# Moving the small steps of the normalisation to GpSimd and splitting the low parts straight from PSUM

## What is computed

```python
h = relu(layernorm(x))                                   # eps 1e-5
D = adj.sum(axis=1);  s = (D + 1e-9) ** -0.5
x = x + relu((adj * s[:, None] * s[None, :]) @ h @ W.T + b)
h = relu(layernorm(x))
g = layernorm(relu(adj @ h @ gcn_w + gcn_b)) * ln_g + ln_b
# mamba(g): 256 inner channels, 16 states
xc, z = split(g @ w_in);  u = silu(conv4(xc) + conv_b)
dbc = u @ w_xp                                           # 8 ranks, 16 B, 16 C
dt = softplus(dbc[:, :8] @ w_dt + b_dt)
h_t = exp(dt * A) * h_(t-1) + dt * B * u                 # along the 8192 rows
y = (sum over states of h_t * C + u * D_skip) * silu(z)
x = x + y @ w_out
```

## Time and profile before

| | us |
|---|---|
| median of 3 runs (lowest, highest) | 2611.35 (2610.81, 2611.61) |
| the profiled execution's own time | 2612.32 |
| its span, first to last instruction | 2610.5 |
| busy: PE / DVE / ACT / POOL | 2222.9 / 2085.1 / 978.6 / 1067.6 |
| chain that ended last | PE 55%, DVE 24%, DMA 8%, issue 8%, ACT 4% |

### The profile page before, as it was taken

How to read it: one execution, slowest core, us unless ns; L and a number is a source line. 1 busy time by engine, 2 the same in 40 slices (tenths; PEclk the granted TensorE clock), 3 DMA queues, 4 the chain that set the end, 5 groups by cost and what they waited for, 6 DMA issues and landing times.

```text
span 2610.5 us, 21684 instructions
## 1 busy us (share of the span) xinstructions
PE 2222.9 (85%) x6736; PEld 1251.9 (48%) x6736; DVE 2085.1 (80%) x2087; ACT 978.6 (37%) x1696; POOL 1067.6 (41%) x461
## 2 busy tenths in 40 slices
PE   0436889999999999999999988889988988886776
PEld 0212334444457888888885434444444443443333
DVE  7899998888527656656652599999999999999997
ACT  0100000000015555555551455555555555555552
POOL 0000000000000000000000499999999999998554
PEclk9968899999999999999999989999999999997898
DMA  9999999989756556555556656665656565562221
GB/s 393 417 421 422 421 418 387 391 360 381 276 214 237 207 201 225 189 215 201 198 181 243 240 202 220 207 215 214 214 204 227 206 223 194 215 210 69 69 73 53
DMA packets 108322, 642.99 MB, mean 246 GB/s; under 512 B 14224, under 2 KB 15024, under 8 KB 42672
## 3 DMA queue, kind: packets, MB, share of 16 engines
q1 hardware_dynamic: 92160, 604.02, 61.4%
q10 hardware_dynamic: 16048, 37.57, 4.0%
HBM read 625.28 MB, written 16.25 MB: 246 GB/s over the span
## 4 chain that ended last, share of the span: by engine, by line
PE 55%; DVE 24%; DMA 8%; issue 8%; ACT 4%; DVEq 0%; ACTq 0%; SPq 0%
PE ps L848 21%; PE ps L767 14%; PE ps L888 10%; DVE ps L685 6%; DVE arena L590 6%; DMA ring<-adj 5%; DVE arena L700 5%; PE ps L966 4%; DVE ring L700 3%; DMA arena<-adj 2%; PE ps L917 2%; PE ps L909 1%; PE ps L970 1%; DVE parts L726 1%; PE ps L928 1%
## 5 line engine op out<-in xcount | busy, mean ns | idle before, releaser
L458 POOL TENSOR_TENSOR rstd<-base,minus_half 128x8 f32<-128x8 f32 (+1 forms) x40 | 84.7, 2118 | 1406.4 <-DVE base L510 811.7
L848 PE MATMUL ps<-adj_parts,h_parts 128*128 128x512 f32 x2592 | 593.6, 390 | 2.6 <-ACT adj_parts L1062 2.2
L888 PE MATMUL ps<-ring,diag_h 128*128 128x512 f32 x1152 | 566.2, 627 | 0.9 <-DVE arena L672 0.9
L848 PEld LDWEIGHTS ps<-adj_parts,h_parts 128*128 128x128 f32 x2592 | 484.7, 188 | 109.0 <-ACT adj_parts L1062 4.7
L590 DVE TENSOR_TENSOR arena<-arena,ring 128x2048 f32<-128x2048 f32 x180 | 412.6, 2292 | 57.9 <-DMA ring<-adj 47.2
L767 PE MATMUL ps<-ring,arena 128*128 128x512 f32 x824 | 381.9, 622 | 53.1 <-DMA ring<-adj 53.0
L474 POOL TENSOR_TENSOR arena<-arena 128x1024 f32<-128x1024 f32 x156 | 377.6, 2431 | 67.7 <-ACT state L1129 67.6
L700 DVE TENSOR_TENSOR_SCAN arena<-arena,state,ps 128x512 f32<-128x512 f32 x312 | 382.4, 1267 | 28.6 <-ACT arena L1137 8.7
L888 PEld LDWEIGHTS ps<-ring,diag_h 128*128 128x128 f32 x1152 | 229.5, 201 | 254.1 <-issue 248.9
L609 DVE TENSOR_TENSOR adj_parts<-ring,adj_parts 128x1024 fp32r<-128x1024 f32 x216 | 264.0, 1225 | 94.5 <-ACT adj_parts L1062 83.7
L1137 ACT ACTIVATE arena<-arena,a_sb 128x512 f32<-128x512 f32 x512 | 338.4, 708 | 0.4
(11 more groups left out here) (97 smaller groups left out, 2095.5 us busy)
## 6 DMA issues: line engine op xcount, KB each, us to landing
ring<-adj SPq DMA_DIRECT2D x452, 1024.0 KB, 6.6
arena<-c_scratch SPq DMA_DIRECT2D x128, 512.0 KB, 4.2
diag_h<-adj SPq DMA_DIRECT2D x32, 1024.0 KB, 12.6
arena<-adj SPq DMA_DIRECT2D x28, 1024.0 KB, 16.1
arena<-x ACTq DMA_DIRECT2D x16, 512.0 KB, 6.0
x_scratch<-arena ACTq DMA_DIRECT2D x8, 512.0 KB, 3.0
arena<-x_scratch ACTq DMA_DIRECT2D x16, 256.0 KB, 5.4
out<-arena ACTq DMA_DIRECT2D x16, 256.0 KB, 3.7
```

The lines of the kernel that those rows point to most:

```text
L848: last = nc.tensor.matmul(acc[:, c, :], h_parts[:, blk % 2, layer, h_part, a * F:(a + 1) * F], adj_parts[:, buf, adj_part, c * MM:(c + 1) ...
L888: last = nc.tensor.matmul((acc_c if i else y_ps)[:, c, :], tile_of(h1, JT * s + a), blk[:, a * STRIP + c * MM:a * STRIP + (c + 1) * MM], s ...
```

## The change

The additive epsilon and the product of minus mean and power leave DVE. POOL now does four steps for a normalisation: minus mean (to `nmr`), variance plus epsilon (to `base`), a wait on its own second step, the power, a wait on its own power, the product. DVE signals `base_ready` from its last `bn_aggr`, and waits for the last `norm_ready` before it overwrites `mv`. The degree's power is as before. The split of the low parts reads `dbc` in PSUM instead of `bcv` in SBUF, and frees the PSUM bank itself; ACT copies `parts` from PSUM too, then only the 32 rows of B and C to `bcv`, and waits for that copy before it issues the DMA of C. PE's waits on `parts_ready` become waits on the freed bank, and dt's matmul waits for ACT's second copy as well.

```diff
-            def power(m, cols):
+            def norm_scale(m, cols):
                 pool.wait_ge(base_ready, m + 1)
...
-                nc.gpsimd.tensor_tensor(rstd[:, 0:cols], base[:, 0:cols], minus_half[:, 0:cols],
-                                        ALU.pow).then_inc(pow_done, 1)
+                nc.gpsimd.tensor_scalar(nmr[:, 0:cols], mv[:, 0:cols, 0], -1.0, None, ALU.mult)
+                nc.gpsimd.tensor_scalar(base[:, 0:cols], mv[:, 0:cols, 1], LN_EPS, None, ALU.add)\
+                    .then_inc(pool_step, 1)
+                pool.wait_ge(pool_step, next(pool_steps))
+                nc.gpsimd.tensor_tensor(rstd[:, 0:cols], base[:, 0:cols], minus_half[:, 0:cols], ALU.pow)\
+                    .then_inc(pow_done, 1)
+                pool.wait_ge(pow_done, m + 1)
+                nc.gpsimd.tensor_tensor(nmr[:, 0:cols], nmr[:, 0:cols], rstd[:, 0:cols], ALU.mult)\
+                    .then_inc(norm_ready, 1)
...
                 step(tile_stats(tiles[taken:], taken))
+                if powers[0]:
+                    dve.wait_ge(norm_ready, powers[0])
                 for t in range(n):
                     ins = nc.vector.bn_aggr(mv[:, t, :], stats[:, t, :])
-                step(ins)
+                ins.then_inc(base_ready, 1)
                 powers[0] += 1
-                nc.vector.tensor_scalar(base[:, 0:n], mv[:, 0:n, 1], LN_EPS, None, ALU.add).then_inc(base_ready, 1)
-            def norm_bias(n):
-                dve.wait_ge(pow_done, powers[0])
-                nc.vector.scalar_tensor_tensor(nmr[:, 0:n], mv[:, 0:n, 0], -1.0, rstd[:, 0:n],
-                                               ALU.mult, ALU.mult).then_inc(norm_ready, 1)
...
                     low = parts[k % 2][LOW:KD, :]
-                    nc.vector.tensor_tensor(low, bcv[LOW:KD, :], low.bitcast(F32), ALU.subtract)\
-                        .then_inc(parts_ready, 1)
+                    nc.vector.tensor_tensor(low, misc_of("dbc", k)[LOW:KD, :], low.bitcast(F32), ALU.subtract)\
+                        .then_inc(misc_free, 1)
...
-                        pe.wait_ge(parts_ready, k + 1)
+                        evacuated(pe, "dbc", k)
+                        pe.wait_ge(c_copied, k + 1)
...
-                    evacuate(("dbc", k), bcv[0:KD, :])
-                    evacuated(act, "dbc", k)
-                    nc.scalar.activation(parts[k % 2][:, :], bcv[0:KD, :], ACT.Copy).then_inc(bc_high, 1)
+                    nc.scalar.activation(parts[k % 2][:, :], misc_of("dbc", k)[0:KD, :], ACT.Copy).then_inc(bc_high, 1)
+                    nc.scalar.activation(bcv[0:2 * DS, :], misc_of("dbc", k)[0:2 * DS, :], ACT.Copy)\
+                        .then_inc(c_copied, 1)
+                    act.wait_ge(c_copied, k + 1)
                     act.dma_start(c_dram[k:k + 1, :].rearrange("a (n t) -> (a n) t", n=DS), bcv[DS:2 * DS, :])\
                         .then_inc(c_out, 16)
```

More of the change, by code:

```diff
@@ L19 @@
+import itertools
 from contextlib import ExitStack
@@ L302, in build @@
         pow_done = sem("pow_done")
+        pool_step = sem("pool_step")
         norm_ready = sem("norm_ready")
@@ L330, in build @@
         bc_high = sem("bc_high")
-        parts_ready = sem("parts_ready")
+        c_copied = sem("c_copied")
         dt_ready = sem("dt_ready")
@@ L448, in _ @@
             nc.gpsimd.memset(state[:, :, :], 0.0).then_inc(consts_done, 1)
-            def power(m, cols):
+            pool_steps = itertools.count(1)
+            def norm_scale(m, cols):
                 pool.wait_ge(base_ready, m + 1)
@@ L457, in power, with degree_scale @@
                     pool.wait_ge(norm_ready, m)
-                nc.gpsimd.tensor_tensor(rstd[:, 0:cols], base[:, 0:cols], minus_half[:, 0:cols],
-                                        ALU.pow).then_inc(pow_done, 1)
-            for m in range(3 * NS):
-                power(m, TPS)
+                nc.gpsimd.tensor_scalar(nmr[:, 0:cols], mv[:, 0:cols, 0], -1.0, None, ALU.mult)
[7 more added lines that the diff above has]
+                    .then_inc(norm_ready, 1)
+            def degree_scale(m):
+                pool.wait_ge(base_ready, m + 1)
+                pool.wait_ge(consts_done, 3)
+                pool.wait_ge(norm_ready, m)
+                nc.gpsimd.tensor_tensor(rstd[:, :], base[:, :], minus_half[:, :], ALU.pow).then_inc(pow_done, 1)
+            for i in range(NS):
+                norm_scale(2 * i, TPS)
+                degree_scale(2 * i + 1)
+            for n in range(NS):
+                norm_scale(2 * NS + n, TPS)
             for g in range(FIRST_SLOT, LAST_SLOT):
@@ L466, in _ @@
                 if normed_chunk is not None:
-                    power(3 * NS + normed_chunk, CT)
+                    norm_scale(3 * NS + normed_chunk, CT)
                 if 0 <= g < NCH * DS:
@@ L584, in _ @@
                         norm_stats([tile_of(xs[i % 2], t) for t in range(TPS)])
-                    if n == 6:
-                        norm_bias(TPS)
                     v = arrived(where)
@@ L644, in complete @@
                     norm_stats(tiles, TPS // 2)
-                if stage == 6:
-                    norm_bias(TPS)
-            for stage in range(7):
+            for stage in range(6):
                 complete(0, stage)
@@ L717, in _ @@
                     norm_stats([gbuf[:, t, :] for t in range(CT)])
-                k = chunk_at(g, NORMALISE)
-                if k is not None:
-                    norm_bias(CT)
                 k = chunk_at(g, SPLIT)
@@ L904, in _ @@
                     kk, nn = divmod(g + 1, DS)
-                    pe.wait_ge(parts_ready, kk + 1)
+                    evacuated(pe, "dbc", kk)
                     if g + 1 >= 2:
@@ L1189, in _ @@
                 if k is not None:
+                    act.wait_ge(misc_full, misc_at["dbc", k] + 1)
                     if k:
-                        act.wait_ge(parts_ready, k)
+                        evacuated(act, "dbc", k - 1)
                         act.wait_ge(c_out, 16 * k)
-                    evacuate(("dbc", k), bcv[0:KD, :])
-                    evacuated(act, "dbc", k)
-                    nc.scalar.activation(parts[k % 2][:, :], bcv[0:KD, :], ACT.Copy).then_inc(bc_high, 1)
+                    nc.scalar.activation(parts[k % 2][:, :], misc_of("dbc", k)[0:KD, :], ACT.Copy).then_inc(bc_high, 1)
+                    nc.scalar.activation(bcv[0:2 * DS, :], misc_of("dbc", k)[0:2 * DS, :], ACT.Copy)\
+                        .then_inc(c_copied, 1)
+                    act.wait_ge(c_copied, k + 1)
                     act.dma_start(c_dram[k:k + 1, :].rearrange("a (n t) -> (a n) t", n=DS), bcv[DS:2 * DS, :])\
```

## The result

| | before | after |
|---|---|---|
| median of 10 runs each, us (lowest, highest) | 2611.57 (2610.56, 2616.17) | 2618.15 (2615.4, 2619.76) |
| profiled execution, its span | 2612.32, 2610.5 | 2618.28, 2616.5 |

What follows compares the result with a forecast made beforehand. DMA bounds stage A and PE stage B; in stage C DVE, POOL and PE are close, with DVE held at POOL's boundaries. +12.0 - 11.6 - 0.7 - 6.3 - 3.4 = -10.0 us, giving 2601 us, range 2590 to 2612.

Steps and rivals of the forecast that it cites:

- Stages A and B: Normalisations outside stage C: longer chain hidden under DMA or PE if in time; 0, at most +2 us.
- Stage A: Normalisation on POOL meets up to three more boundaries of DVE's adds, some 7 us; result wanted a strip later; 0.
- The split: Low parts, slot 11 of stage C: one input in PSUM, 0.67 us each for 16, -11.6 us.
- The steps on POOL in stage C: Three more steps before slot 15's product: 1.0 us for a round, bounds 0.5 and 1.6.
- The later boundary: Gate multiplication on DVE, slot 5 of stage C, ends 1.0 us later in each of twelve rounds: +12.0 us.
- The gate's mean: DVE's 128x1024 multiplication L748 in stage C: mean rises from 1.67 to about 3.0 us.
- DVE's waits for PE in slots 3 to 9: Stage C: 11 waits, 6.3 us in all, vanish as PE starts earlier and DVE comes later: -6.3 us.
- The mean round: Round of 16 slots in stage C: 70.8 us, from 71.52 over twelve rounds.
- POOL's waits in the first leg: POOL's waits for ACT around slot 7, in the leg from slot 13: stay near 0.3 us.
- The sum for stage C: Stage C terms: +12.0 - 11.6 - 0.7 - 6.3 - 3.4 = -10.0 us.
- The rivals: Stage C: DVE's gain whole, 2591, 0.18; POOL bounds, 2618, 0.10; split blocked, 2612.5, or PE's waits stay, 2607, 0.15.
- POOL as the bound: Stage C: small steps cost 1.01 us each, POOL's round becomes 72.55 us; +7, 2618 us; chance 0.10.

Runs made afterwards that it cites:

- the two slots tried here: Gate multiplication in slot 22 instead of 21: 2595.49 us with split and POOL's steps in C (before 2600.37), 2608.01 us with split alone (before 2600.25).

## Why the prediction was wrong

**Stages A and B, the step that failed.** It said: "In B, its latency grows by 1 us at most; PE's next need lies some 2 us behind it at both hand-overs. 0, at most +2 us." There are six hand-overs, where the step had looked at two; the latency grew by 1.8 us; and the slack I had read, some 2 us, was not there: ACT had 0.34 us to spare and PE, already waiting 0.37, none. B cost 14.8 us: six waits 1.5 us longer, and 5.5 us of matmuls at the lower clock behind four of them. I had read B's window with PE busy for 65.00 of 65 us as a sign of cover. It is the reverse: an engine that is never idle has nothing to give, and where its supplier is held up beyond its own slack just before it delivers, PE stands. It is not the busy share alone, though: with ACT's waiting activations three pieces further back, the same chain cost no such wait. The step priced the length of the chain, and did not ask what stands behind the waiting instruction in ACT's list.

**Stage A.** "some 7 us, in a strip of about 80 us whose result is wanted a strip later". The 4.7 us were within this, and the result was indeed not wanted. But behind the activation in ACT's list stands the issue of a load, and at one place, where SP's loads stood waiting for PE, a load issued 4.7 us late left the DMA engines without work. +3.0 us for the kernel, 1.8 of it in stage A. The share of 1.01 that I had read the earlier trace rows is of one window; the six later loads, as late, cost nothing more.

**The split.** -11.6 us was forecast, at 0.67 us each. Measured were 0.695 us each and -11.0 us for the kernel. Right, with its reason: one input in PSUM, no wait for POOL. (The prediction counted L510 among the instructions with two SBUF inputs. It is a TENSOR_SCALAR with one, and was held all the same: 0.87 us, where it takes 0.17 unblocked.)

**The steps on POOL in stage C.** One scaling took 0.23 us (0.3 forecast), the product 0.20 to 0.26 (0.35), and the block grew by 0.9 us in place of 1.0. The Trainium skill (GPSIMD Engine Reference, Engine selection) was quoted for a factor of two against VectorE; the Trainium skill gives it for two inputs, and the prediction doubled L510 with it, which has one. For one input and 8 columns the rows show 0.17 us on VectorE and 0.27 to 0.33 at 844 us on POOL; for two inputs and 4 columns L514 takes 0.14 to 0.16 unblocked and POOL's product 0.20, less than the factor. The estimate of 1.2 us for the three steps with their waits was too high, since they took some 0.8, and stage C could bear the steps.

**The later boundary.** The gate's mean was to be "about 3.0" us: it is 2.96 in nine of the twelve rounds and 2.49 over all 16. w was to be about 2.0 and is 1.76. DVE's waits for PE in slots 3 to 9 are "nearly gone", 1.2 us of 6.4. The mean round was to be 70.8 and is 71.04. One sign missed: POOL's waits in the first leg were to stay near 0.3 us, and they are gone in eleven of the twelve rounds; POOL now waits only where a round begins, so the first leg is as long as its own list. The sum for stage C, -10.0, stands against -10.8 measured by the kernel with both parts in C only.

**The rivals.** POOL as the bound gave 2618, which is the measured time, but for a reason that did not happen: POOL's steps took 0.2 us and not 1.01, and it still waits for ACT, 10.5 us in the rounds. That the number came out is luck. None of the rivals lay outside stage C. That was the second fault: the slower rival was sought where all the reading had been done.

## What to carry to other kernels

Work that is taken from a full engine and put on an idle one makes the chain of a hand-over longer, also in those stages where neither of the two is the bound. Before such a move, list for every stage the instruction that waits for the chain, what stands behind it in the order of its engine (a DMA issue counts), and how long the bound engine's idle time there already is: where it is not zero, what the chain is longer beyond the slack of the waiting engine lands once for each hand-over, 1.5 of 1.8 us here. If the move is wanted, set the waiting instruction further back in its engine's list; that made the kernel 14.4 us faster here, 11.3 of them in stage B.

Where two engines share a port, an instruction's wait depends on the point at which it meets the other's list. So try the neighbouring slots after every change of either list: of the two slots tried here, each version had the other as its better one.

## What was not expected of the hardware

**Idle work made the kernel faster.** Two scalings without use, some 0.3 us each with their gap, took 6.0 us off 2600.4. 3.6 us of it lie in the rounds, where they moved POOL's boundaries against the gate.

**A port is free between an instruction and one that waits for it.** A gap of 0.08 us on POOL was enough for a DVE multiplication to go through with 1.20 us, and POOL's next then took 3.26. The Trainium skill (SBUF — State Buffer, Who interferes with whom) has an exclusive lock for the whole instruction, and the order of issue decides who is held; these rows agree, 2.95 us behind a POOL instruction and 1.20 ahead of one.

**The clock.** An idle time of 1.89 us on PE was followed by a granted clock of 0.83 over the next 10 us at four hand-overs and by 1.00 at two, with the same idle time. What differs between them was not found. With the steps on POOL in stage B only, it was the same four hand-overs. Idle times of 0.37 us at the same places never had it. It made a lost 1.5 us into 2.4 in the mean.
